# Fusing the recurrent r and z products of a GRU step into one product per column group

## The chip, the cores and the metric

The kernel runs on one core of a Trainium2 chip. The metric is the device time of one execution in microseconds; lower is better. Names of engines in what follows: PE is the matrix engine (its weight loads are listed apart, as PEld), DVE the vector engine, ACT the scalar engine, POOL the general engine, SP the engine that issues the DMAs.

## What is computed

The input `x` has 8 sequences of 512 positions and 256 channels. A mixture-of-experts layer with one shared and eight routed experts is added to it, and then a GRU-like recurrence runs over the 512 positions, whose outputs are added too:

```
x = x + moe(x, cond, ...)                 # per token, no recurrence
for t in range(512):                       # H is 8 x 256, H = cond at the start
    Z = sigmoid(x_t @ Wxz.T + bxz + H @ Whz.T + bhz)
    R = sigmoid(x_t @ Wxr.T + bxr + H @ Whr.T + bhr)
    H_tilda = tanh(x_t @ Wxh.T + bxh + (R * H) @ Whh.T + bhh)
    H = Z * H + (1 - Z) * H_tilda
    Y_t = H @ Whq.T + bhq
out = x + Y
```

The products with `x_t` need no earlier state and can be made a tile ahead. The products with `H` and `R * H` cannot: a step needs the state of the step before, and within a step the third product needs the first.

## The kernel before

The 512 positions are cut into NT = 32 tiles of TS = 16 steps. Two things run interleaved on the same engines. One is the recurrence, 512 steps in a row. The other is all the rest of the next tiles (experts up and down, routing, input projections) and the output product of the tile before; it is cut into small pieces, and tables written out by hand (`DOWNS1`, `UP_GAP2`, `ADD2`, `SILU1`, `HIDDEN1`, `BIASED1`, `ROUTE_AHEAD1` and others, indexed by a place r from 0 to 31 in a period of two tiles) say after which part of which step each piece is issued. Every engine has its own instruction stream in program order, and semaphores tie them together.

A state is 8 sequences by 256 channels. The channels are cut into NG = 4 groups of GW = 64, and each group sits in its own 32 partitions, of which 8 (B) are used. So r, z and c of one step are each a 128-partition by 64-column block of a PSUM bank, of which `NI` = 2 halves of Q = 32 columns are taken in turn by ACT and DVE. The step in program order:

- PE: `gate_product(r_ps, 0, hT, k)` for k = 0, 1 (the 256 channels of H are two contractions of 128), with 4 matmuls of 64 columns each, one for a column group of the array; it writes bank `r_bank`. Then the same for z into the first 64 columns of `zc_bank`. Then `fill_up`, a piece of the other work. Then, after a wait for `rhT_ready`, the same for c into columns 64 to 127 of `zc_bank`. Then `fill_rest`, more other work. All are made by line 1247. A float32 matmul is two records in the trace, so 8 matmuls show as 16 records. Where there is no other work left, `keep_busy` (line 1255) puts two matmuls there whose result nobody reads.
- ACT: tanh of r in two halves (`t_r`, line 693), tanh of z (`t_z`, line 695), the seed of the next step's r (`seed_r`, line 616: a copy of the precomputed input part from `xs` into `r_bank`, onto which the products accumulate), then `a_row` (line 704), an affine copy of `t_z` which waits for `tz_ready`. After c is done: tanh of c in two halves (`t_h`, line 713), then `seed_zc` (line 624), the seed of the next step's z and c, 128 columns. Then one piece of other work.
- DVE: transposes `t_r` (line 982, twice), makes `rhT` from it (line 985, twice), transposes `a_row` into `factors` (line 990), then a piece of other work in some steps, then `terms` from `factors` (line 1001), then transposes `t_h` into `terms` (line 1006, twice) and makes the new state with a scan into `hist` (line 1009, twice). Then another piece of other work in most steps.

Every tile ACT also copies the finished states (`keep_states`, line 631) right behind `a_row` of the tile's first step. SP stores and reloads the input parts by way of DRAM; two of its waits count the seeds of z and c, to know when the rows of `xs` may be overwritten. PSUM has 8 banks of 512 float32 columns, all used.

Of the kernel before, what the change touches and what calls it, by code (L numbers as in the profile page):

```python
# [17 lines left out]
def moe_then_gru(nc, x, cond, router_w, router_b, w1, w3, w2, we1, we2,  # L18
# [32 lines left out]
    with ctx:  # L51
# [84 lines left out]

        r_bank = ctx.enter_context(nc.psum_tensor("r_bank", [P, 512], F32))
        zc_bank = ctx.enter_context(nc.psum_tensor("zc_bank", [P, 512], F32))
        up_ps = [ctx.enter_context(nc.psum_tensor(f"up_ps{i}", [P, 512], F32)) for i in range(2)]
        dn_ps = [ctx.enter_context(nc.psum_tensor(f"dn_ps{i}", [P, 512], F32)) for i in range(2)]  # L140
        misc = ctx.enter_context(nc.psum_tensor("misc", [P, 512], F32))
        aux = ctx.enter_context(nc.psum_tensor("aux", [P, 512], F32))
        r_ps, z_ps, c_ps = r_bank[:, 0:GW], zc_bank[:, 0:GW], zc_bank[:, GW:2 * GW]
        tr_ps = [r_bank, zc_bank]

# [47 lines left out]
        xs_zeroed = sem("xs_zeroed")  # L193
        seeded_r = sem("seeded_r")
        seeded_zc = sem("seeded_zc")
        w13_high_ready = sem("w13_high_ready")
# [5 lines left out]
        hT_ready = sem("hT_ready")  # L202
        r_done = sem("r_done")
        z_done = sem("z_done")
        c_done = sem("c_done")
# [201 lines left out]
        def _(sp):  # L407
# [99 lines left out]
            def body(n, scan, proj, outs):  # L507
                if n % 2 == 0 and n > 0:
                    store_out(n - 2)
                if proj:  # L510
                    sp.wait_ge(xs_second, 16 * NG * (n + 1))
                    for q in range(PIECES):
                        store_inputs(n + 1, q)
                    sp.wait_ge(seeded_zc, TS * n + HALF)
                    for q in range(PIECES):
                        sp.wait_ge(xp_stored[q], 16 * (n + 2))
                        gate_rows(q, 0, xs_first)
                if n % 2 == 0 and 0 < n < NT:
                    store_out(n - 1)
                if proj:  # L520
                    sp.wait_ge(seeded_zc, TS * (n + 1))
# [35 lines left out]
        def _(act):  # L557
# [121 lines left out]
            act.wait_ge(xs_first, 16 * NG)  # L679
            seed_r(0, 0)  # L680
            seed_zc(0, 0)
            consume_up(1, 2)

            def body(n, scan, proj, outs):
                for s in range(TS):
# [3 lines left out]
                    if scan:  # L689
                        for i in range(NI):  # L690
                            if i == 0:
                                act.wait_ge(r_done, TS * n + s + 1)
                            act.activation(t_r[:, i, :], r_ps[:, i * Q:(i + 1) * Q], ACT.Tanh, scale=0.5).then_inc(tr_ready, 1)  # L693
                        act.wait_ge(z_done, TS * n + s + 1)
                        act.activation(t_z[:, :, :].rearrange("p i q -> p (i q)"), z_ps, ACT.Tanh, scale=0.5).then_inc(tz_ready, 1)
                    if after:
                        if s + 1 == HALF:
                            act.wait_ge(xs_second, 16 * NG * (n + 1))
                        if last:
                            act.wait_ge(xs_first, 16 * NG * (n + 2))  # L700
                        seed_r(*after)
                    if scan:
# [13 lines left out]
                    if after:  # L716
                        seed_zc(*after)
                    if 0 <= p < NPAIR and r in first_or(p, UP_ACT2_FIRST, UP_ACT2):
# [311 lines left out]
        def _(pe):  # L1030
# [41 lines left out]
            def set_bits():  # L1072

                pe.wait_ge(tr_act, (NTR + 1) // 2)
                pe.wait_ge(tr_dve, NTR // 2)
                for ps in (r_bank, zc_bank):

# [251 lines left out]
            def body(n, scan, proj, outs):  # L1329
                for s in range(TS):  # L1330
# [3 lines left out]
                    if scan:  # L1334
                        if (n, s) == (0, 0):
                            pe.wait_ge(seeded_r, 1)
# [44 lines left out]
```

## Time and profile before

| | us |
|---|---|
| median of 3 runs | 1278.86 |
| lowest and highest | 1277.06, 1281.6 |
| the profiled execution, its own time | 1277.44 |
| its span, first to last instruction | 1275.5 |
| granted clock of PE, share of full | 1.00 |
| PE matmul, PE weight load busy | 1249.8, 890.8 |
| DVE, ACT busy | 997.2, 803.3 |

The span holds a head of some 51 us, in which weights are loaded, split and transposed, and then the 512 steps until 1271 us. Busy time of PE counts a matmul from its first column to the write of its last, and matmuls overlap; so it says that something was in the array, not that the array was fed without a gap.

### The profile page before, as it was taken

Reading aid. Unit: us, or ns where it says so; the run is one execution under the profiler, and the core shown is the slowest. Engines: PE = TensorE matmul, PEld = TensorE weight load, DVE = VectorE, ACT = ScalarE, POOL = GpSimd, SP = SyncE. Lnnn points to the kernel's source line nnn. Section 1 sums busy time; section 2 is a strip of 40 time slices with the busy share of each in tenths; the row PEclk is TensorE's granted clock in tenths of the full one; section 3 lists DMA queues with packets and bytes.
Section 4 is the critical chain, followed back from the end, with each engine's and each line's share of the span. In section 5 each row is a group of like instructions: output and inputs, shape, how many; then the busy total and the mean of one; then the engine's idle time right before and its main releaser. Section 6 shows DMA issues by size and latency. Waiting matters only on the chain.

```text
span 1275.5 us, 84499 instructions
## 1 busy us (share of the span) xinstructions
PE 1249.8 (98%) x35704; PEld 890.8 (70%) x35704; DVE 997.2 (78%) x6111; ACT 803.3 (63%) x4402; POOL 7.4 (1%) x25
## 2 busy tenths in 40 slices
PE   9999999999999999999999999999999999999887
PEld 8877677766677776667776667776667776666554
DVE  6678888788787888878888787887877787877765
ACT  4366666666666666666666666666666666666554
POOL 1000000000000000000000000000000000000000
PEclk9999999999999999999999999999999999999999
DMA  8211011111101111011111101111011111001110
GB/s 273 57 36 43 24 38 30 42 41 34 36 24 39 38 37 45 24 37 27 44 39 35 38 21 41 35 39 45 27 33 27 44 39 33 23 21 27 33 32 11
DMA packets 76186, 51.34 MB, mean 40 GB/s; under 512 B 40609, under 2 KB 73761, under 8 KB 75809
## 3 DMA queue, kind: packets, MB, share of 16 engines
q1 hardware_dynamic: 75128, 45.29, 13.7%
q8 instruction: 281, 4.60, 1.5%
q14 instruction: 97, 0.79, 0.2%
q10 hardware_dynamic: 680, 0.66, 0.2%
HBM read 29.13 MB, written 16.78 MB: 36 GB/s over the span
## 4 chain that ended last, share of the span: by engine, by line
PE 93%; DVE 3%; ACT 2%; issue 1%; DMA 1%; SPq 0%
PE dn_ps L1083 27%; PE up_ps L1111 26%; PE zc_bank L1247 21%; PE r_bank L1247 14%; PE aux L1083 2%; DVE terms L1006 2%; PE dn_ps L1119 1%; ACT t_h L713 1%; PE misc L1083 1%; DVE hist L1009 1%; DMA x_all<-in_L_cond_W1e 1%; DVE t_rT L982 1%; ACT t_r L693 0%; DVE rhT L985 0%; SPq L411 0%
## 5 line engine op out<-in xcount | busy, mean ns | idle before, releaser
L982 DVE STREAM_TRANSPOSE t_rT<-t_r 128x32 f32<-128x32 f32 x1024 | 156.2, 191 | 171.1 <-ACT t_r L693 163.6
L693 ACT ACTIVATE t_r<-r_bank 128x32 f32<-128x32 f32 x1024 | 146.1, 195 | 210.2 <-PE r_bank L1247 200.2
L713 ACT ACTIVATE t_h<-zc_bank 128x32 f32<-128x32 f32 x1024 | 145.9, 195 | 207.7 <-PE zc_bank L1247 207.7
L1083 PE MATMUL dn_ps<-we_sb,x_all 128*32 128x256 f32 (+1 forms) x5144 | 274.5, 329 | 0.0
L1247 PEld LDWEIGHTS zc_bank<-whT,rhT 128*8 128x8 f32 x8192 | 118.1, 87 | 177.5 <-DVE rhT L985 176.9
L1247 PE MATMUL r_bank<-whT,hist 128*8 128x64 f32 x8192 | 210.1, 220 | 16.0 <-DVE hist L1009 13.4
L1247 PE MATMUL zc_bank<-whT,rhT 128*8 128x64 f32 x8192 | 211.0, 220 | 2.8 <-DVE rhT L985 0.3
L1247 PE MATMUL zc_bank<-whT,hist 128*8 128x64 f32 x8192 | 208.9, 219 | 0.8 <-issue 0.8
L1006 DVE STREAM_TRANSPOSE terms<-t_h 128x32 f32<-128x32 f32 x1024 | 156.5, 192 | 38.2 <-ACT t_h L713 19.7
L1247 PEld LDWEIGHTS r_bank<-whT,hist 128*8 128x8 f32 x8192 | 117.6, 88 | 94.6 <-DVE hist L1009 72.5
L1083 PEld LDWEIGHTS dn_ps<-we_sb,x_all 128*32 128x32 f32 x5144 | 137.9, 110 | 31.9 <-issue 1.0
L1111 PE MATMUL up_ps<-x_high,we_high 128*128 128x256 f32 (+1 forms) x540 | 159.1, 295 | 0.2 <-DVE hid L820 0.2
L1111 PE MATMUL up_ps<-x_high,we_low 128*128 128x256 f32 (+1 forms) x540 | 155.4, 288 | 0.0
L1111 PE MATMUL up_ps<-x_low,we_high 128*128 128x256 f32 x526 | 154.9, 294 | 0.0
L624 ACT ACTIVATE zc_bank<-gru_raw 128x128 f32<-128x128 f32 x512 | 144.3, 282 | 16.0
L1009 DVE TENSOR_TENSOR_SCAN hist<-factors,terms 128x16 f32<-128x16 f32 x1024 | 145.4, 184 | 0.0
L1247 PEld LDWEIGHTS zc_bank<-whT,hist 128*8 128x8 f32 x8192 | 142.4, 90 | 0.2
L990 DVE STREAM_TRANSPOSE factors<-a_row 128x64 f32<-128x64 f32 x512 | 126.0, 246 | 19.5 <-ACT a_row L704 1.4
L985 DVE SCALAR_TENSOR_TENSOR rhT<-t_rT,hist 128x8 f32<-128x8 f32 x1024 | 133.3, 168 | 0.0
L704 ACT ACTIVATE a_row<-t_z 128x64 f32<-128x64 f32 x512 | 125.7, 245 | 0.0
L852 DVE SCALAR_TENSOR_TENSOR x_all<-dn_ps,gates_all,x_all 128x256 f32<-128x256 f32 x256 | 121.3, 474 | 5.6 <-PE dn_ps L1119 1.9
L616 ACT ACTIVATE r_bank<-gru_raw 128x64 f32<-128x64 f32 x512 | 114.3, 223 | 3.4 <-DMA gru_raw<-gate_inputs_by_group 3.4
(132 smaller groups left out, 1691.4 us busy)
## 6 DMA issues: line engine op xcount, KB each, us to landing
gate_inputs_by_group<-gru_raw SPq DMA_DIRECT2D x64, 192.0 KB, 2.0
gru_raw<-gate_inputs_by_group SPq DMA_DIRECT2D x256, 48.0 KB
xT_all<-in_x SPq DMA_DIRECT2D x448, 8.0 KB
x_all<-in_x SPq DMA_DIRECT2D x31, 128.0 KB
out<-gru_raw SPq DMA_DIRECT2D x31, 128.0 KB
x_all<-in_L_cond_W1e SPq DMA_DIRECT2D x4, 512.0 KB, 7.6
we_sb<-in_L_cond_W2e SPq DMA_DIRECT2D x4, 512.0 KB, 8.6
xT_all<-in_L_cond_w SPq DMA_DIRECT2D x2, 256.0 KB, 5.3
```

Source lines behind the costliest of these rows:

```text
L624: act.activation(zc_bank[:, 0:2 * GW], xs[:, s, GW:RW], ACT.Copy).then_inc(seeded_zc, 1)
L693: act.activation(t_r[:, i, :], r_ps[:, i * Q:(i + 1) * Q], ACT.Tanh, scale=0.5).then_inc(tr_ready, 1)
L704: act.activation(a_row[:, :, :], t_z[:, :, :], ACT.Copy, bias=0.5, scale=-0.5).then_inc(a_ready, 1)
L713: act.activation(t_h[:, i, :], c_ps[:, i * Q:(i + 1) * Q], ACT.Tanh, scale=-1.0).then_inc(th_ready, 1)
L982: dve.transpose(t_rT[:, i, :], t_r[:, i, :]).then_inc(trT_done, 1)
L985: dve.scalar_tensor_tensor(rhT[:, i, :], t_rT[:, i, 0:B], 1.0, old[:, i, :], ALU.add, ALU.mult)\
L990: dve.transpose(factors[:, :, :, 1].rearrange("p i q -> p (i q)"), a_row[:, :, :].rearrange("p i q -> p (i q)"))\
L1006: dve.transpose(terms[:, i, :, 0], t_h[:, i, :]).then_inc(thT_done, 1)
L1009: dve.tensor_tensor_scan(hist[:, s, i, :, :].rearrange("p b e -> p (b e)"), factors[:, i, 0:B, :].rearrange("p b e -> p (b e)"), terms[:, ...
L1083: done = pe.matmul(ps[Q * j:Q * (j + 1), col:col + cols], lhsT[:, Q * j:Q * (j + 1)], rhs, start=first, stop=last, tile_position=(0, Q * j ...
L1111: done = pe.matmul(up_ps[place % 2][:, half * PAIR + begin * P:half * PAIR + end * P], w, (x_low if low_x else x_high)[:, p % 2, begin:end ...
L1247: done = pe.matmul(ps[Q * j:Q * j + B, :], lhsT[:, k, :], whT[:, gate, k, j * GW:(j + 1) * GW], start=False, stop=(k == NI - 1), tile_posi ...
```

## The change

The z block moves out of the bank that it shared with c and lies beside r: `rz_bank` holds r in columns 0 to 63 and z in 64 to 127, and `c_bank` holds c alone. The two products of 64 columns per column group and contraction half become one of 128 columns (its moving operand is two runs of 64 from `whT`). The seeds follow the banks: `seed_rz` copies 128 columns, `seed_c` 64, at the places where `seed_r` and `seed_zc` were. The product writes both gates, so there is one semaphore for them (`rz_done`), and the seed that overwrites both waits for both tanhs.

```
-        r_ps, z_ps, c_ps = r_bank[:, 0:GW], zc_bank[:, 0:GW], zc_bank[:, GW:2 * GW]
+        r_ps, z_ps, c_ps = rz_bank[:, 0:GW], rz_bank[:, GW:2 * GW], c_bank[:, 0:GW]
...
-            def seed_r(n, s):
+            def seed_rz(n, s):
                 if (n, s) == (0, 0):
                     act.wait_ge(bits_set, 2)
                 else:
                     act.wait_ge(tr_ready, NI * (TS * n + s))
-                act.activation(r_ps, xs[:, s, 0:GW], ACT.Copy).then_inc(seeded_r, 1)
+                    act.wait_ge(tz_ready, TS * n + s)
+                act.activation(rz_bank[:, 0:2 * GW], xs[:, s, 0:2 * GW], ACT.Copy).then_inc(seeded_rz, 1)
...
-            def seed_zc(n, s):
+            def seed_c(n, s):
...
-                act.activation(zc_bank[:, 0:2 * GW], xs[:, s, GW:RW], ACT.Copy).then_inc(seeded_zc, 1)
+                act.activation(c_ps, xs[:, s, 2 * GW:RW], ACT.Copy).then_inc(seeded_c, 1)
...
                             if i == 0:
-                                act.wait_ge(r_done, TS * n + s + 1)
+                                act.wait_ge(rz_done, TS * n + s + 1)
                             act.activation(t_r[:, i, :], r_ps[:, i * Q:(i + 1) * Q], ACT.Tanh, scale=0.5).then_inc(tr_ready, 1)
-                        act.wait_ge(z_done, TS * n + s + 1)
                         act.activation(t_z[:, :, :].rearrange("p i q -> p (i q)"), z_ps, ACT.Tanh, scale=0.5).then_inc(tz_ready, 1)
...
                         for k in range(NI):
                             pe.wait_ge(hT_ready, g + k + 1)
-                            done = gate_product(r_ps, 0, hT, k)
-                        done.then_inc(r_done, 1)
-                        pe.wait_ge(seeded_zc, TS * n + s + 1)
-                        for k in range(NI):
-                            done = gate_product(z_ps, 1, hT, k)
-                        done.then_inc(z_done, 1)
+                            for j in reversed(range(NG)):
+                                done = pe.matmul(rz_bank[Q * j:Q * j + B, 0:2 * GW], hT[:, k, :], whT[:, 0:2, k, j * GW:(j + 1) * GW],
+                                                 start=False, stop=(k == NI - 1), tile_position=(0, Q * j), skip_group_check=True)
+                        done.then_inc(rz_done, 1)
                     fill_up(p, r, scan)
                     if scan:
                         for k in range(NI):
                             pe.wait_ge(rhT_ready, g + k + 1)
                             if k == 0:
-                                pe.wait_ge(tz_ready, TS * n + s + 1)
+                                pe.wait_ge(seeded_c, TS * n + s + 1)
                             done = gate_product(c_ps, 2, rhT, k)
```

SP's two waits on `seeded_zc` become waits on `seeded_c` with the same counts; the names of the banks are exchanged where the head uses them for transposes.

## Rows read from the trace of the kernel before

**Rows 1.** Page, part 1: busy us (share of the span) and instructions
```profile
PE 1249.8 (98%) x35704; PEld 890.8 (70%) x35704; DVE 997.2 (78%) x6111; ACT 803.3 (63%) x4402; POOL 7.4 (1%) x25
```
**Rows 2.** Waits of the whole span: total us, times, longest us
```profile
ACT t_h L713 <- PE zc_bank L1247: 207.7, 481, 0.8
ACT t_r L693 <- PE r_bank L1247: 200.2, 379, 0.8
PEld zc_bank L1247 <- DVE rhT L985: 176.9, 509, 0.6
DVE t_rT L982 <- ACT t_r L693: 163.6, 434, 1.5
PEld r_bank L1247 <- DVE hist L1009: 72.5, 221, 1.0
```
**Rows 3.** Timeline, 627.7 to 630.0 us, one step: start us, length us, engine, line
```profile
627.70 0.41 PE L1247 MATMUL r_bank<-whT,hist 128*8 128x64 f32 x16
...
627.92 0.41 PE L1247 MATMUL zc_bank<-whT,hist 128*8 128x64 f32 x16
...
628.15 0.83 PE L1083 MATMUL dn_ps<-we_sb,x_all 128*32 128x256 f32 x16
628.17 0.28 ACT L693 ACTIVATE t_r<-r_bank 128x32 f32<-128x32 f32 x2 [0.60 <-PE r_bank L1247]
628.40 0.22 ACT L695 ACTIVATE t_z<-zc_bank 128x64 f32<-128x64 f32 x1
628.40 0.30 DVE L982 STREAM_TRANSPOSE t_rT<-t_r 128x32 f32<-128x32 f32 x2 [0.29 <-ACT t_r L693]
628.52 0.22 ACT L616 ACTIVATE r_bank<-gru_raw 128x64 f32<-128x64 f32 x1
628.65 0.26 DVE L985 SCALAR_TENSOR_TENSOR rhT<-t_rT,hist 128x8 f32<-128x8 f32 x2
628.66 0.25 ACT L704 ACTIVATE a_row<-t_z 128x64 f32<-128x64 f32 x1
...
628.87 0.41 PE L1247 MATMUL zc_bank<-whT,rhT 128*8 128x64 f32 x16
628.94 0.25 DVE L990 STREAM_TRANSPOSE factors<-a_row 128x64 f32<-128x64 f32 x1
629.11 0.13 DVE L776 TENSOR_TENSOR hit<-hit,rank 128x16 f32<-128x16 f32 x1
...
629.28 0.17 DVE L777 TENSOR_REDUCE best<-hit 128x2 f32<-128x16 f32 x1
...
629.35 0.28 ACT L713 ACTIVATE t_h<-zc_bank 128x32 f32<-128x32 f32 x2 [0.44 <-PE zc_bank L1247]
...
629.48 0.18 DVE L1001 SCALAR_TENSOR_TENSOR terms<-factors,hist 128x16 f32<-128x16 f32 x1
...
629.58 0.31 DVE L1006 STREAM_TRANSPOSE terms<-t_h 128x32 f32<-128x32 f32 x2
...
629.83 0.28 DVE L1009 TENSOR_TENSOR_SCAN hist<-factors,terms 128x16 f32<-128x16 f32 x2
```
**Rows 4.** Groups by form, whole span: busy us, mean ns of one record
```profile
L1247 PE MATMUL r_bank<-whT,hist 128*8 128x64 f32 x8192 | 210.1, 220 | 16.0 <-DVE hist L1009 13.4
...
L693 ACT ACTIVATE t_r<-r_bank 128x32 f32<-128x32 f32 x1024 | 146.1, 195 | 210.2 <-PE r_bank L1247 200.2
...
L1083 PE MATMUL dn_ps<-we_sb,x_all 128*32 128x128 f32 x2448 | 123.1, 273 | 0.0
...
L1083 PE MATMUL dn_ps<-wxT,x1T 128*32 128x384 f32 x992 | 103.0, 486 | 0.0
```
**Rows 5.** Timeline of ACT, 661.0 to 663.6 us, a step with `keep_states`
```profile
661.73 0.22 ACT L695 ACTIVATE t_z<-zc_bank 128x64 f32<-128x64 f32 x1
661.85 0.22 ACT L616 ACTIVATE r_bank<-gru_raw 128x64 f32<-128x64 f32 x1
661.99 0.25 ACT L704 ACTIVATE a_row<-t_z 128x64 f32<-128x64 f32 x1
662.14 0.64 ACT L631 ACTIVATE gru_raw<-hist 128x256 f32<-128x256 f32 x1
662.69 0.27 ACT L713 ACTIVATE t_h<-zc_bank 128x32 f32<-128x32 f32 x2
662.99 0.28 ACT L624 ACTIVATE zc_bank<-gru_raw 128x128 f32<-128x128 f32 x1
663.21 0.37 ACT L580 ACTIVATE gru_raw<-up_ps 128x256 f32<-128x256 f32 x1
```
**Rows 6.** Timeline of DVE: no wide operation, `shared_silu`, `shared_silu` at r = 9, two routing operations
```profile
653.07 0.17 DVE L1001 SCALAR_TENSOR_TENSOR terms<-factors,hist 128x16 f32<-128x16 f32 x1
653.35 0.31 DVE L1006 STREAM_TRANSPOSE terms<-t_h 128x32 f32<-128x32 f32 x2
...
724.57 0.16 DVE L1001 SCALAR_TENSOR_TENSOR terms<-factors,hist 128x16 f32<-128x16 f32 x1
724.73 0.30 DVE L1006 STREAM_TRANSPOSE terms<-t_h 128x32 f32<-128x32 f32 x2
...
660.41 0.16 DVE L1001 SCALAR_TENSOR_TENSOR terms<-factors,hist 128x16 f32<-128x16 f32 x1
660.53 0.31 DVE L1006 STREAM_TRANSPOSE terms<-t_h 128x32 f32<-128x32 f32 x2
...
631.87 0.18 DVE L1001 SCALAR_TENSOR_TENSOR terms<-factors,hist 128x16 f32<-128x16 f32 x1
631.96 0.31 DVE L1006 STREAM_TRANSPOSE terms<-t_h 128x32 f32<-128x32 f32 x2
```
**Rows 7.** Windows: the middle and a stretch without other work; busy us, then PEclk
```profile
200.00:1100.00 900.00, 896.82 (x26420) 636.80 (x26415) 723.40 (x4512) 584.81 (x3234) 0.00 (x0) 1.00 0.14 35
1235.00:1260.00 25.00, 20.12 (x566) 13.37 (x566) 15.82 (x108) 13.71 (x86) 0.00 (x0) 1.00 0.03 9
```

More of the change, by code:

```diff
@@ L135, in moe_then_gru @@
         hist = sb("hist", [P, TS, NI, B, 2])
-        r_bank = ctx.enter_context(nc.psum_tensor("r_bank", [P, 512], F32))
-        zc_bank = ctx.enter_context(nc.psum_tensor("zc_bank", [P, 512], F32))
+        rz_bank = ctx.enter_context(nc.psum_tensor("rz_bank", [P, 512], F32))
+        c_bank = ctx.enter_context(nc.psum_tensor("c_bank", [P, 512], F32))
         up_ps = [ctx.enter_context(nc.psum_tensor(f"up_ps{i}", [P, 512], F32)) for i in range(2)]
@@ L142, in moe_then_gru @@
         aux = ctx.enter_context(nc.psum_tensor("aux", [P, 512], F32))
-        r_ps, z_ps, c_ps = r_bank[:, 0:GW], zc_bank[:, 0:GW], zc_bank[:, GW:2 * GW]
-        tr_ps = [r_bank, zc_bank]
+        r_ps, z_ps, c_ps = rz_bank[:, 0:GW], rz_bank[:, GW:2 * GW], c_bank[:, 0:GW]
+        tr_ps = [rz_bank, c_bank]
         by_group = nc.dram_tensor("gate_inputs_by_group", [NG, P, RW], F32, kind="Internal").ap()
@@ L193, in moe_then_gru @@
         xs_zeroed = sem("xs_zeroed")
-        seeded_r = sem("seeded_r")
-        seeded_zc = sem("seeded_zc")
+        seeded_rz = sem("seeded_rz")
+        seeded_c = sem("seeded_c")
         w13_high_ready = sem("w13_high_ready")
@@ L202, in moe_then_gru @@
         hT_ready = sem("hT_ready")
-        r_done = sem("r_done")
-        z_done = sem("z_done")
+        rz_done = sem("rz_done")
         c_done = sem("c_done")
@@ L513, in body @@
                         store_inputs(n + 1, q)
-                    sp.wait_ge(seeded_zc, TS * n + HALF)
+                    sp.wait_ge(seeded_c, TS * n + HALF)
                     for q in range(PIECES):
@@ L520, in body @@
                 if proj:
-                    sp.wait_ge(seeded_zc, TS * (n + 1))
+                    sp.wait_ge(seeded_c, TS * (n + 1))
                     for q in range(PIECES):
@@ L679, in _ @@
             act.wait_ge(xs_first, 16 * NG)
-            seed_r(0, 0)
-            seed_zc(0, 0)
+            seed_rz(0, 0)
+            seed_c(0, 0)
             consume_up(1, 2)
@@ L700, in body @@
                             act.wait_ge(xs_first, 16 * NG * (n + 2))
-                        seed_r(*after)
+                        seed_rz(*after)
                     if scan:
@@ L716, in body @@
                     if after:
-                        seed_zc(*after)
+                        seed_c(*after)
                     if 0 <= p < NPAIR and r in first_or(p, UP_ACT2_FIRST, UP_ACT2):
@@ L1075, in set_bits @@
                 pe.wait_ge(tr_dve, NTR // 2)
-                for ps in (r_bank, zc_bank):
+                for ps in (rz_bank, c_bank):
                     pe.matmul(ps[:, 0:2 * GW], zeros[:, :], zeros[:, 0:2 * GW], start=True, stop=True).then_inc(bits_set, 1)
@@ L1335, in body @@
                         if (n, s) == (0, 0):
-                            pe.wait_ge(seeded_r, 1)
+                            pe.wait_ge(seeded_rz, 1)
                         for k in range(NI):
                             pe.wait_ge(hT_ready, g + k + 1)
-                            done = gate_product(r_ps, 0, hT, k)
-                        done.then_inc(r_done, 1)
-                        pe.wait_ge(seeded_zc, TS * n + s + 1)
-                        for k in range(NI):
-                            done = gate_product(z_ps, 1, hT, k)
-                        done.then_inc(z_done, 1)
+                            for j in reversed(range(NG)):
+                                done = pe.matmul(rz_bank[Q * j:Q * j + B, 0:2 * GW], hT[:, k, :], whT[:, 0:2, k, j * GW:(j + 1) * GW],
+                                                 start=False, stop=(k == NI - 1), tile_position=(0, Q * j), skip_group_check=True)
+                        done.then_inc(rz_done, 1)
                     fill_up(p, r, scan)
```

## The prediction

> **What bounds the kernel now.** The page's first part comes first, and it misleads: PE is busy 98% of the span, and DVE and ACT 78% and 63% [rows 1]. The waits say otherwise. PE's weight loader waited 509 times, once in nearly every one of the 512 steps, for `rhT` before the c product, 176.9 us in all; ACT waited 481 times for c and DVE 434 times for `t_r` [rows 2]. So the engines wait for each other in a ring. The timeline of one step gives the ring its numbers [rows 3]: r product starts at 627.70; `t_r` 628.17 (0.47 later); its transpose 628.40 (0.23); `rhT` 628.65 (0.25); c product 628.87 (0.22); `t_h` 629.35 (0.48); its transpose 629.58 (0.23); scan 629.83 (0.25). The next r product starts 0.24 to 0.25 behind the scan, since the ring from c to r costs 1.20 by the same kind of links. Sum: 1.17 from r to c and 1.20 from c to r, 2.37 to 2.38 us for a step. 512 steps of 2.38 are 1219 us, and with the head of 51 us and the last outputs this is the whole span. No link in the ring waits for anything but the one before it. The z product and the piece of other work stand on PE between r and c, and both fit: z runs from 627.92, the piece from 628.15, and c still starts 0.22 behind `rhT`, as it does in other steps. So z costs nothing today: it is streamed while ACT and DVE work on r.
>
> **Part 1: r is released later.** In the merged product the last record of r is also the last of z. How long is one pass? A record of 64 columns lasts 220 ns (by its name 128x64), one of 128 columns 273, one of 384 columns 486 [rows 4]. From 128 to 384 columns 213 ns are added in four steps of 64 columns: 53 ns for every 64 columns. The 16 records of r are four passes one after the other (four column groups of the array run beside each other): the r product starts at 627.70 and z at 627.92 [rows 3], so a pass of 64 columns takes 0.22 / 4 = 0.055 us. The merged product has four passes too (its 16 records are 2 halves of the contraction x 2 records x 4 groups), each 53 ns longer. Three lie before the last pass and the last is itself longer: 4 x 53.4 = 213.6 ns until `rz_done`. This is the z product, moved from behind the release of r to before it. Nothing in the ring gives it back, since `t_r` starts as soon as PE is done, and so do the transpose, `rhT` and c. 512 x 0.2136 = **109.4 us slower**. Bounds: if the two runs of 64 in the moving operand cost nothing more, that is the value; at 0.220 (the full length of four passes of 64, [rows 3]) it is 112.6, and at 4 x 0.0527 it is 107.9. No gain hides here unless PE itself were late for c in some steps, and 509 waits of 512 say that it is not [rows 2].
>
> What PE saves is small. The 16 weight-load and 16 matmul records of z go, but the columns stay: eight passes of 0.055 become four of 0.109, 0.44 us both. At most 0.01 us a step, and PE is not what the step waits for: nothing.
>
> The Trainium skill (TensorE: Matmul & The Clock Gate, Single matmul latency and Back-to-back issue gap) counts one cycle of 2.4 GHz for a column, 27 ns for 64 more, and a fixed 2.5 ns for every matmul, measured for bf16. By that page's figure the delay would be an estimated 4 x 27 = 107 ns a step and 55 us in all. This case's rows show 53 ns for 64 float32 columns in one record, so the trace disagrees and is used.
>
> **Part 2: the seed stands in the way of `a_row`.** ACT's order behind `t_r` is `t_z`, the next seed, `a_row`. Before, `t_z` starts 0.23 behind `t_r`, the seed of r 0.12 behind `t_z` without waiting for it, and `a_row`, which waits until `t_z` is written, 0.26 to 0.27 behind `t_z`: 0.49 behind `t_r` [rows 3, 5]. After, `t_z` has no wait and can follow at the pitch of two 32-column halves. That pitch is 0.28 - 0.195 = 0.09 (the pair takes 0.28 [rows 3], one 0.195 [rows 4]), so `t_z` is at 0.09 + 0.09 = 0.19. The seed covers both gates and must now wait until `t_z` is written, the same 0.265: it starts at 0.45. `a_row` follows a 128-column seed. The row nearest to that is ACT's other 128-column seed, from which the next instruction starts 0.22 later (662.99 to 663.21, [rows 5]). So `a_row` starts at 0.67 in place of 0.49, **0.18 later** against `t_r`. If the pitch grows only by the 64 columns that the seed has more (0.12 from `t_z` to the seed in rows 5, plus 0.05) it is 0.17 and the delay 0.14; if `t_z` doesn't come forward, the delay is 0.22. I take 0.18 and keep 0.14 and 0.22.
>
> Who waits? `factors` waits for `a_row` (628.66 to 628.94), the pieces of other work on DVE stand behind `factors`, `terms` (L1001) behind those, and the transpose of `t_h` (L1006) behind that. L1006 is in the ring. DVE can take it from 0.09 behind L1001's start (631.87 to 631.96 [rows 6], the least seen; 0.10 in rows 3). So the slack of a step is its distance from L1001 to L1006 less 0.09, and the loss is 0.18 less the slack. By kind of step:
> - Two routing operations between (r = 26 to 31, in 14 pairs of tiles: 84 steps): distance 0.10 or less, slack about 0.005 [rows 3]. 84 x 0.175 = 14.7 us.
> - `shared_silu` at r = 9 (15 steps): distance 0.12, slack 0.03 [rows 6]. 15 x 0.15 = 2.3 us.
> - One wide operation between (`shared_silu`, `shared_hidden` or `add_output_bias` at r = 3, 4, 5, 7, 11, 12, 19: seven places in 15 pairs, 105 steps): distance 0.16, slack 0.07 [rows 6]. 105 x 0.11 = 11.5 us.
> - Steps with none or one small operation: distance 0.28 and more, slack 0.19 [rows 6]. Nothing.
> - First steps of every second tile, where `keep_states` stands behind `a_row` and ends just in time: L631 at 662.14, `t_h` 0.55 behind it, with no wait for PE [rows 5]. It moves by 0.18 with `a_row`; 15 such steps, the others are among the routing steps above. 15 x 0.17 = 2.6 us.
>
> Sum **31 us**. At 0.14 it is some 21, at 0.22, where also the steps with a slack of 0.19 lose, some 44.
>
> **Part 3: what costs nothing.** The seed of c is 64 columns in place of 128, so ACT is free 0.05 us sooner behind `t_h`; it then has 0.2 us more than before until `t_r`, so nobody sees it. PE no longer waits for a seed between r and z, and its c product waits for `seeded_c`, which was issued a whole half step earlier (the seed follows `t_h` of the step before). SP's two waits get the same counts at nearly the same time, and the transfers behind them have half a tile to land. The pieces of other work on DVE and ACT behind the scan get 0.2 us more room; they delay nothing in the ring today, so nothing is gained.
>
> **Sum.** 1277.4 (the profiled execution; its span 1275.5) + 109.4 + 31 = 1418 us. That execution is 1.4 us below the median of the runs shown, so 1418 to 1419; I say 1418. A step goes from 2.38 to about 2.59 us, and to 2.77 in routing steps.
>
> **The rivals.**
> - *The ring alone.* The seed's detour stays within DVE's slack, because DVE can take `t_h`'s transpose later without loss or because ACT passes `a_row` sooner. Then only part 1 stands: 1277.4 + 109.4 = 1387, with a little of part 2 up to 1398. For it: most steps have 0.19 slack. Against: in 84 steps nothing is left between L1001 and L1006 [rows 3].
> - *Faster: PE is the bound.* If the 98% of rows 1 were a real limit, 16 fewer weight loads and 16 fewer matmul records a step would count. Eight passes of 0.055 to 0.056 become four of 0.109, at best 0.012 us a step, 6 us: 1271. It decides where PE's pieces end later than `rhT`; in this trace they ended before it in 509 of 512 steps [rows 2]. The Trainium skill (Perfetto Trace Analysis, Identifying the Most-Contended Engine) says that matmul busy time is a poor measure and that weight-load busy time is the better; here that is 70% [rows 1], and the waits agree with it.
> - *The clock falls.* PE idles about 0.22 us more in each step, before c. If the granted level went from 2.4 to 1.2 GHz, every pass of the ring would double: r and z 0.44, c 0.22 more a step and the pieces no longer fit, well over 1700. Against it: from 1235 to 1260 us there is no other work, PE's matmul records cover only 20.12 of 25 us and its weight loads 13.37, and the granted clock is 1.00, the level of 2.4 GHz [rows 7]. In the changed kernel the middle would be fuller than that.
> - *It doesn't do what it says.* If DVE or ACT were the bound already, moving r by 0.21 would be hidden in steps where `t_r` was late for another reason. 379 waits of ACT for r are counted [rows 2], fewer than 512; if the other 133 hid all of it, part 1 would be 81 us and the total 1389. The step starts don't support that: 0.47 from r to `t_r` [rows 3] is just three passes of 0.055, a record of 0.22 and some 0.08.
>
> **How the numbers follow.** My case as worked out, 1399 to 1432: 75%. The ring alone or hidden in part, 1380 to 1398: 14%. More than 1432 (part 2 at its upper bound with something queued behind it, or the clock): 8%. PE as the bound, 1271: 2%, and another 1% for anything within 0.3% of 1277, which is about what a measurement of this kernel can tell from no change. The range takes the first case and most of the second: 1392 to 1434.
>
> **What the changed kernel's profile would show.** The merged product's records last 273 ns, and `t_r` starts 0.68 behind its start in place of 0.47; r to c is 1.39 in place of 1.17. If it is 1.17, part 1 is wrong. c to r is 1.20 in steps without wide work on DVE; in routing steps it is 1.37 with L1001 and L1006 0.09 apart. If it is 1.20 everywhere, part 2 is wrong. `a_row` starts 0.67 behind `t_r`. PEld's wait for `rhT` grows by about 0.2 us a step, some 100 us. A granted clock below 1.00 would undo all of it.

## The result, and the profile after

The changed kernel takes 1424.5 us (median of 4 runs, 1423.6 to 1429.8) where the kernel before takes 1278.6 (4 runs): a ratio of 1.1146, 95% interval 1.1129 to 1.1163. It is 146 us slower. The profiled execution has a span of 1421.8 us.

Part 1 of its page answers rows 1. PE is busy for a smaller share (92%, its weight loads 62%) and has 8192 matmuls and 8192 weight loads fewer, which brought nothing:

```profile
PE 1309.2 (92%) x27512; PEld 883.8 (62%) x27512; DVE 967.7 (68%) x6111; ACT 835.8 (59%) x4402; POOL 7.4 (1%) x25
```

The waits (line that waited, line that released it, total us, times, longest) answer rows 2:

```profile
ACT t_r L693 <- PE rz_bank L1339: 378.2, 512, 1.2
PEld c_bank L1246 <- DVE rhT L984: 291.7, 512, 0.8
DVE t_rT L981 <- ACT t_r L693: 280.9, 510, 1.7
PEld rz_bank L1339 <- DVE hist L1008: 121.7, 367, 1.0
DVE factors L989 <- ACT a_row L703: 121.2, 483, 0.5
ACT t_h L712 <- PE c_bank L1246: 102.3, 459, 0.5
```

ACT now waits for the product in all 512 steps, 378 us against 200. The fifth line is new: `factors` waits for `a_row` in 483 steps, where before it waited in 3 of them, 1.4 us in all. That is part 2 of the prediction in one line. The same line of the kernel before:

```profile
DVE factors L990 <- ACT a_row L704: 1.4, 3, 1.0
```

One step with routing operations, as a timeline (start, length, engine, line), answers rows 3:

```profile
781.30 0.62 PE L1339 MATMUL rz_bank<-whT,hist 128*8 128x128 f32 x16 [0.16 <-DVE hist L1008]
...
781.74 0.83 PE L1082 MATMUL dn_ps<-we_sb,x_all 128*32 128x128 f32 x16
781.99 0.28 ACT L693 ACTIVATE t_r<-rz_bank 128x32 f32<-128x32 f32 x2 [0.35 <-PE rz_bank L1339]
782.16 0.23 ACT L694 ACTIVATE t_z<-rz_bank 128x64 f32<-128x64 f32 x1
782.22 0.31 DVE L981 STREAM_TRANSPOSE t_rT<-t_r 128x32 f32<-128x32 f32 x2 [0.88 <-ACT t_r L693]
782.47 0.26 DVE L984 SCALAR_TENSOR_TENSOR rhT<-t_rT,hist 128x8 f32<-128x8 f32 x2
782.48 0.28 ACT L616 ACTIVATE rz_bank<-gru_raw 128x128 f32<-128x128 f32 x1
...
782.69 0.41 PE L1246 MATMUL c_bank<-whT,rhT 128*8 128x64 f32 x16
782.70 0.24 ACT L703 ACTIVATE a_row<-t_z 128x64 f32<-128x64 f32 x1
782.97 0.24 DVE L989 STREAM_TRANSPOSE factors<-a_row 128x64 f32<-128x64 f32 x1 [0.24 <-ACT a_row L703]
...
783.16 0.29 ACT L712 ACTIVATE t_h<-c_bank 128x32 f32<-128x32 f32 x2 [0.22 <-PE c_bank L1246]
...
783.51 0.17 DVE L1000 SCALAR_TENSOR_TENSOR terms<-factors,hist 128x16 f32<-128x16 f32 x1
...
783.60 0.30 DVE L1005 STREAM_TRANSPOSE terms<-t_h 128x32 f32<-128x32 f32 x2
...
784.09 0.29 PE L1339 MATMUL rz_bank<-whT,hist 128*8 128x128 f32 x3
```

Product to `t_r` is 0.69 (0.47 before), product to c 1.39 (1.17), both as forecast. From `t_r` on to c nothing changed: 0.23, 0.25, 0.22. Behind c, `t_h` is 0.47 later (0.48 before), but its transpose stands 0.44 behind it, not 0.23, right behind `terms`, which is right behind the routing operations, `factors` and `a_row`. So c to the next product is 1.40 here against 1.20, and the step 2.79.

The form of the merged product answers rows 4 (count, busy us, mean ns):

```profile
L1339 PE MATMUL rz_bank<-whT,hist 128*8 128x128 f32 x8192 | 319.3, 274 | 42.3 <-DVE hist L1008 27.5
```

Taken over all steps of the two traces, the mean distance from the first product to c went from 1.177 to 1.387 (210 ns, 107.5 us in all), and that from c to the next step's first product from 1.205 to 1.281 (76 ns, 38.9 us; the expectations below have it as 38.7). Together 146 us. These two numbers are what the experiments have to account for.

### The profile page after: what moved, and what is told of

It is laid out like the page before. It is cut to its first block, busy times and chain, and to the rows that moved or that the text cites. A ratio compares the mean times of both kernels' runs of the same rounds, so it can differ in the third digit from the quotient of the medians.

```text
span 1421.8 us, 68563 instructions
## 1 busy us (share of the span) xinstructions
PE 1309.2 (92%) x27512; PEld 883.8 (62%) x27512; DVE 967.7 (68%) x6111; ACT 835.8 (59%) x4402; POOL 7.4 (1%) x25
## 4 chain that ended last, share of the span: by engine, by line
PE 49%; DVE 24%; ACT 20%; issue 5%; DMA 1%; ACTq 0%; SPq 0%; DVEq 0%
PE rz_bank L1339 23%; PE up_ps L1110 13%; ACT t_r L693 9%; PE c_bank L1246 7%; DVE t_rT L981 5%; ACT rz_bank L616 5%; DVE terms L1005 4%; DVE factors L989 4%; ACT a_row L703 3%; DVE hist L1008 3%; DVE terms L1000 2%; ACT t_z L694 2%; DVE rhT L984 2%; PE aux L1082 2%; PE dn_ps L1082 2%
## 5 line engine op out<-in xcount | busy, mean ns | idle before, releaser
L693 ACT ACTIVATE t_r<-rz_bank 128x32 f32<-128x32 f32 x1024 | 146.2, 195 | 378.2 <-PE rz_bank L1339 378.2
L1339 PE MATMUL rz_bank<-whT,hist 128*8 128x128 f32 x8192 | 319.3, 274 | 42.3 <-DVE hist L1008 27.5
L1246 PEld LDWEIGHTS c_bank<-whT,rhT 128*8 128x8 f32 x8192 | 117.1, 87 | 291.7 <-DVE rhT L984 291.7
L1246 PE MATMUL c_bank<-whT,rhT 128*8 128x64 f32 x8192 | 209.9, 220 | 64.1 <-DVE rhT L984 7.8
L1339 PEld LDWEIGHTS rz_bank<-whT,hist 128*8 128x8 f32 x8192 | 171.9, 89 | 131.0 <-DVE hist L1008 121.7
L712 ACT ACTIVATE t_h<-c_bank 128x32 f32<-128x32 f32 x1024 | 145.5, 194 | 104.4 <-PE c_bank L1246 102.3
L616 ACT ACTIVATE rz_bank<-gru_raw 128x128 f32<-128x128 f32 x512 | 143.9, 281 | 51.9 <-DMA gru_raw<-gate_inputs_by_group 3.6
L624 ACT ACTIVATE c_bank<-gru_raw 128x64 f32<-128x64 f32 x512 | 116.7, 228 | 16.0
L694 ACT ACTIVATE t_z<-rz_bank 128x64 f32<-128x64 f32 x512 | 118.8, 232 | 0.0
L1110 PEld LDWEIGHTS up_ps<-x_high,we_high 128*128 128x128 f32 x540 | 101.6, 188 | 12.4 <-DVE hid L819 0.3
```

Of the source, the lines that this page charges most:

```text
L616: act.activation(rz_bank[:, 0:2 * GW], xs[:, s, 0:2 * GW], ACT.Copy).then_inc(seeded_rz, 1)
L1110: done = pe.matmul(up_ps[place % 2][:, half * PAIR + begin * P:half * PAIR + end * P], w, (x_low if low_x else x_high)[:, p % 2, begin:end ...
L1246: done = pe.matmul(ps[Q * j:Q * j + B, :], lhsT[:, k, :], whT[:, gate, k, j * GW:(j + 1) * GW], start=False, stop=(k == NI - 1), tile_posi ...
L1339: done = pe.matmul(rz_bank[Q * j:Q * j + B, 0:2 * GW], hT[:, k, :], whT[:, 0:2, k, j * GW:(j + 1) * GW], start=False, stop=(k == NI - 1), ...
```

## Experiments

The theory on trial: a ring of latencies sets the time; it is longer by the z product, behind which r is now released (part 1), and by `a_row`, which the seed holds up (part 2). The rivals: the merged product or its bank is the cost; DVE would have hidden the order on ACT; PE's stream is the bound.

### The order on ACT

e1_arow_first:

```
                         act.activation(t_z...).then_inc(tz_ready, 1)
+                    if scan:
+                        act.wait_ge(tz_ready, TS * n + s + 1)
+                        act.activation(a_row...).then_inc(a_ready, 1)
                     if after:
...
                         seed_rz(*after)
-                    if scan:
-                        act.wait_ge(tz_ready, TS * n + s + 1)
-                        act.activation(a_row...).then_inc(a_ready, 1)
```

> The changed kernel with a_row issued ahead of the seed of r and z, everything else kept. Theory (ring plus detour): the 38.7 us by which c to r is longer than before come from a_row standing behind a seed that waits for t_z. With a_row first it starts 0.17 + 0.27 = 0.44 behind t_r (0.49 before the change, 0.71 after it), so these 38.7 us go. In 31 steps keep_states now stands behind the 128-column seed and starts 0.80 instead of 0.64 behind t_r, 31 x 0.15 = 4.7 us. 1424.5 - 38.7 + 4.7 = 1390 us. Rival (c to r is longer because the merged product or the banks disturb it, not the order on ACT): no change, 1424 us. Rival (DVE's slack would have hidden the order anyway and all is part 1): no change either.

Measured: 1390.3 us (ratio to before 1.0869, 1.0852 to 1.0885). Its timeline of ACT:

```profile
742.86 0.29 ACT L693 ACTIVATE t_r<-rz_bank 128x32 f32<-128x32 f32 x2 [0.87 <-PE rz_bank L1339]
743.03 0.23 ACT L694 ACTIVATE t_z<-rz_bank 128x64 f32<-128x64 f32 x1
743.30 0.26 ACT L697 ACTIVATE a_row<-t_z 128x64 f32<-128x64 f32 x1
743.46 0.26 ACT L616 ACTIVATE rz_bank<-gru_raw 128x128 f32<-128x128 f32 x1
```

`a_row` is 0.44 behind `t_r`, and 34 us are gone by swapping two instructions. Over all steps c to r comes back to 1.214 on average; what is left of part 2, 4.5 us, stands in the first steps of the tiles, where `keep_states` now follows the wider seed. Part 2 is shown: it was the order, and DVE did not hide it.

e2_one_wait, on the changed kernel:

```
                 else:
-                    act.wait_ge(tr_ready, NI * (TS * n + s))
                     act.wait_ge(tz_ready, TS * n + s)
```

> The changed kernel; the seed of r and z waits for t_z alone (which comes behind t_r on the same engine), so the separate wait instruction ahead of it is gone. Theory: the seed starts 0.265 behind t_z instead of 0.324, a_row 0.65 behind t_r instead of 0.71, which is 0.16 later than before the change instead of 0.22. By the slacks of the steps, which overstate the changed kernel's loss a little (44 worked out for 38.7 measured), the loss falls from 44 to 26: some 15 to 18 us less, 1407 to 1409 us. Rival (the second wait is free, the seed's delay has another cause): 1424 us.

Measured: 1407.9 us (1.101, 1.0992 to 1.1029), 16.6 less than the changed kernel. Where two waits are written ahead of one instruction, the trace has a semaphore instruction of its own for one of them. The changed kernel's trace lists it for line 615, the wait for `t_z`, in 511 steps (only 63 such in the kernel before):

```profile
L615 ACTq EVENT_SEMAPHORE  x511: 17/17/38, 51.9 to 1413.1; - x171
```

The first wait written (`tr_ready`) is carried by the seed itself, the second stands ahead of it. Here the second is the one that ends last, and the seed starts 0.32 behind `t_z` (782.16 to 782.48 above). With one wait it is 0.26:

```profile
900.31 0.23 ACT L693 ACTIVATE t_z<-rz_bank 128x64 f32<-128x64 f32 x1
900.57 0.28 ACT L615 ACTIVATE rz_bank<-gru_raw 128x128 f32<-128x128 f32 x1
900.79 0.24 ACT L702 ACTIVATE a_row<-t_z 128x64 f32<-128x64 f32 x1
```

This is the part of part 2 that the prediction did not have.

e6_seed_detour puts part 2 alone on the kernel before:

```
                     act.wait_ge(tr_ready, NI * (TS * n + s))
-                act.activation(r_ps, xs[:, s, 0:GW], ACT.Copy).then_inc(seeded_r, 1)
+                    act.wait_ge(tz_ready, TS * n + s)
+                act.activation(r_bank[:, 0:2 * GW], xs[:, s, 0:2 * GW], ACT.Copy).then_inc(seeded_r, 1)
```

> The kernel before, in which the seed of r is 128 columns wide and waits for t_z too, as in the change; 64 of its columns are never read. r is released as before. So this is part 2 alone, and larger than in the change, since t_z still comes 0.223 behind t_r: seed at 0.223 + 0.324, a_row 0.216 behind it, 0.76 instead of 0.49, 0.27 later. By the slacks of the steps this costs 61 to 66 us, and 5% less if it overstates as for the change: 1338 to 1344 us, with steps up to 0.27 longer where DVE has routing operations and 0.08 longer in the others. Rival (DVE hides it): 1279 us.

Measured: 1334.8 us (1.0432, 1.0416 to 1.0447), 54 us above before where 58 to 63 were expected with the 5% taken off. In all steps of its trace the distance from r to c has the mean 1.179, that of before (1.177), and from c to r 1.318 instead of 1.205, which is 57 us in all. The slacks alone had given 61 to 66, so they read 6 to 15% high. Two reasons are in the trace: where one wide operation stands ahead of `terms`, the transpose follows `terms` by 0.08, not 0.09 as assumed, and the scan follows the transpose by 0.240 (median) in place of 0.248.

### When r is released

e4_r_waits_for_z, on the kernel before:

```
                                 act.wait_ge(r_done, TS * n + s + 1)
+                                act.wait_ge(z_done, TS * n + s + 1)
                             act.activation(t_r[:, i, :], ...).then_inc(tr_ready, 1)
-                        act.wait_ge(z_done, TS * n + s + 1)
                         act.activation(t_z...)
```

> The kernel before, in which the tanh of r also waits for the z product; products, banks and seeds are as before. Theory (the time went because r is released with z, not because the product is merged): t_r starts 0.224 later in every step, 512 x 0.224 = 115 us, and a_row is not late, so nothing is added: 1278.6 + 115 = 1393 us, 7 us above e3 because two products of 64 columns take 0.01 us longer than one of 128. Rival (the wider product itself, its two runs or its bank, costs the time): 1279 us.

Measured: 1424.7 us (1.1138, 1.1122 to 1.1155): 32 us more than expected, and by chance the time of the changed kernel. The expectation failed by the same mechanism as above. The order of the two waits puts the late one, for z, in an instruction of its own, in every step:

```profile
L693 ACTq EVENT_SEMAPHORE  x512: 17/17/17, 51.5 to 1415.9; - x171
```

and from the first product to `t_r` it is 0.76, as the timelines of PE and of ACT show:

```profile
901.67 0.41 PE L1247 MATMUL r_bank<-whT,hist 128*8 128x64 f32 x16
901.90 0.41 PE L1247 MATMUL zc_bank<-whT,hist 128*8 128x64 f32 x16
```

ACT, same step:

```profile
902.43 0.28 ACT L694 ACTIVATE t_r<-r_bank 128x32 f32<-128x32 f32 x2 [0.59 <-PE zc_bank L1247]
```

e9_r_waits_for_z_alone has the one wait only (against the kernel before):

```
-                                act.wait_ge(r_done, TS * n + s + 1)
+                                act.wait_ge(z_done, TS * n + s + 1)
                             act.activation(t_r[:, i, :], ...).then_inc(tr_ready, 1)
-                        act.wait_ge(z_done, TS * n + s + 1)
                         act.activation(t_z...)
```

> As e4_r_waits_for_z, but the tanh of r waits for the z product only, with no second wait beside it. In e4 r to t_r was 0.760 us, 0.06 more than the 0.224 of z accounts for, and the wait for z stood in a semaphore instruction of its own ahead of t_r. Theory (that separate instruction, when its wait ends last, costs 0.06 in every step, 31 us): 1424.7 - 31 = 1393 us, r to c 1.40. Rival (a z product in the way costs 0.06 by itself): 1425 us.

Measured: 1391.3 us (1.0877, 1.0861 to 1.0893). Products of 64 columns, banks and seeds of the kernel before, and yet 112 us slower, only because r is handed on with z: r to c is 1.398 on average, c to r stays at 1.205. The merged product as such is not the cost.

e3_seeds_behind_th moves the seed of r and z from ahead of `a_row` to behind `t_h`, on the changed kernel:

```
-                    if after:
...
-                        seed_rz(*after)
                     if scan:
                         act.wait_ge(tz_ready, TS * n + s + 1)
...
                     if after:
...
+                        seed_rz(*after)
                         seed_c(*after)
...
-                        if (n, s) == (0, 0):
-                            pe.wait_ge(seeded_rz, 1)
+                        pe.wait_ge(seeded_rz, TS * n + s + 1)
                         for k in range(NI):
                             pe.wait_ge(hT_ready, g + k + 1)
```

> The changed kernel with the seed of r and z moved behind t_h, beside the seed of c, and PE waiting for it in every step. Theory: a_row is as in e1_arow_first and keep_states goes back to its old place, so part 2 is gone altogether: 1424.5 - 38.7 = 1386 us, which is before plus the delay of r alone (1278.6 + 107.5). The seed must be done within 0.72 us of t_h; it stands 0.19 behind it and takes 0.28, so PE does not wait for it. Rival (it does wait): each step grows by what it is late.

Measured: 1429.6 us (1.1177, 1.1158 to 1.1197), a miss of 44 us. The scan to the product was 0.34 in place of 0.25:

```profile
900.61 0.29 ACT L616 ACTIVATE rz_bank<-gru_raw 128x128 f32<-128x128 f32 x1
...
900.91 0.28 DVE L1007 TENSOR_TENSOR_SCAN hist<-factors,terms 128x16 f32<-128x16 f32 x2
...
901.25 0.62 PE L1337 MATMUL rz_bank<-whT,hist 128*8 128x128 f32 x16
```

The seed had ended at 900.90, as the scan began, so it was not late. The view of what the product waits for names it all the same ("ACT rz_bank L616: 85.1, 219"), which is a case of a release read off wrongly. e10_state_wait_first turns the two waits round (the edit against e3):

```
-                        pe.wait_ge(seeded_rz, TS * n + s + 1)
                         for k in range(NI):
                             pe.wait_ge(hT_ready, g + k + 1)
+                            if k == 0:
+                                pe.wait_ge(seeded_rz, TS * n + s + 1)
```

> As e3_seeds_behind_th, but PE's wait for the new state is written ahead of its wait for the seed. In e3 the scan to the product was 0.337 us instead of 0.246, with the wait for the state in a semaphore instruction of its own ahead of the first weight load. Theory (the late wait has to be the one that the weight load carries; the other, long over, costs nothing): 1429.6 - 512 x 0.091 = 1383 us, at most 1386. Rival (the seed is really late for PE): 1430 us as in e3.

Measured: 1383.6 us (1.082, 1.0804 to 1.0836). The 0.09 is gone (scan to product: mean 0.340 in e3, 0.248 here, 0.249 in the kernel before):

```profile
900.17 0.28 DVE L1007 TENSOR_TENSOR_SCAN hist<-factors,terms 128x16 f32<-128x16 f32 x2
...
900.42 0.34 PEld L1338 LDWEIGHTS rz_bank<-whT,hist 128*8 128x8 f32 x16 [0.27 <-DVE hist L1007]
900.42 0.62 PE L1338 MATMUL rz_bank<-whT,hist 128*8 128x128 f32 x16
```

This kernel is the change without part 2: its c to r is 1.203 on average, that of before. It is the best form of the merged product that was tried, and still 104 us slower than the kernel before: moving the seeds does not touch part 1.

### Columns or instructions

e5_no_z leaves the z product out of the kernel before:

```
-                        for k in range(NI):
-                            done = gate_product(z_ps, 1, hT, k)
-                        done.then_inc(z_done, 1)
```

The tanh of z waits for `seeded_zc` in place of `z_done`, and so does the c product.

> The kernel before without the z product (z is the tanh of its seed alone, so the state is another); all else is kept. It takes 16 weight loads and 16 matmul records, 0.22 us of PE's stream, out of every step, many more than the merge does. Theory (a ring of latencies, PE has room): nothing moves, 1277 to 1280 us. Rival (PE's stream is the bound, so that a merge saves time there): up to 512 x 0.22 = 115 us faster, 1164 us.

Measured: 1280.9 us against 1280.5, a ratio of 1.0008 (0.9997 to 1.0019). Two things cancel in that, and the trace keeps them apart. Up to 1230 us the granted clock is 1.00; in the last 40 us it falls:

```profile
1200.00:1230.00 30.00, 23.35 (x536) 12.84 (x524) 21.42 (x135) 16.84 (x105) 0.00 (x0) 1.00 0.11 32
1255.00:1272.00 17.00, 15.51 (x222) 9.72 (x218) 9.52 (x66) 8.30 (x52) 0.00 (x0) 0.60 0.04 10
```

The first 489 steps, all at the full clock, take 1162.8 us against 1165.3 before; the last 22 take 57.0 against 52.2. So with 16 matmul and 16 weight-load records a step less, PE gains at most 3 us where the rival asked for 115. That PE's stream is the bound is refuted.

e7_96_columns, on the changed kernel:

```
-  pe.matmul(rz_bank[Q * j:Q * j + B, 0:2 * GW], hT[:, k, :], whT[:, 0:2, k, j * GW:(j + 1) * GW], ...)
+  pe.matmul(rz_bank[Q * j:Q * j + B, 0:GW + Q], hT[:, k, :], whT[:, 0:2, k, j * GW:j * GW + 48], ...)
```

> The changed kernel with the merged product cut from 128 to 96 columns (48 of each gate's weights per group, so it computes something else); instructions and seeds are kept. Theory (columns cost, 53.4 ns for 64 in a pass): each of four passes is 26.7 ns shorter, 0.107 us a step, 54.7 us: 1370 us. Rival (the number of instructions costs): 1424 us.

Measured: 1376.0 us (1.0751, 1.0731 to 1.077), 48.5 less than the changed kernel and 6 above the expectation. The granted clock was not 1.00 to the end. Windows of this kernel (busy us of PE, PEld, DVE, ACT, POOL, then the clock):

```profile
1300.00:1313.00 13.00, 10.86 (x232) 5.50 (x224) 9.08 (x59) 7.46 (x43) 0.00 (x0) 1.00 0.05 18
1313.00:1346.00 33.00, 29.66 (x412) 18.24 (x412) 16.77 (x114) 15.91 (x92) 0.00 (x0) 0.60 0.09 24
1352.00:1370.00 18.00, 16.54 (x226) 10.21 (x218) 9.08 (x63) 8.53 (x51) 0.00 (x0) 0.59 0.03 9
```

e12_96_columns_busier doubles `keep_busy`:

```
-                for k in range(KC):
-                    done = pe.matmul(up_ps[0][:, 0:PAIR], w1_high[:, k, 0:P], x_high[:, 0, :, k, :], ...)
+                for k in range(2 * KC):
+                    done = pe.matmul(up_ps[0][:, 0:PAIR], w1_high[:, k % KC, 0:P], x_high[:, 0, :, k % KC, :], ...)
```

> As e7_96_columns, with four instead of two matmuls in each keep_busy, which stands only where no other work is left. In e7 the granted clock fell to half in two stretches of the last 60 us, and e7 took 1376 us where 1370 was worked out. Theory (those stretches are the 6 us): the clock stays at full and it is 1370 us, with the columns term at 0.107 us a step. Rival (the clock is not the cause, the columns term was too large): 1376 us; or the longer keep_busy delays c, which would be over 1376 us.

Measured: 1369.2 us (1.0712, 1.0694 to 1.073), and the same window of its profiled execution:

```profile
1313.00:1346.00 33.00, 29.44 (x545) 20.29 (x538) 19.31 (x132) 18.34 (x106) 0.00 (x0) 1.00 0.09 24
```

So 32 columns less, with as many instructions in the merged product, are worth 1424.5 - 1369.2 = 55 us, 0.108 us a step. The trace agrees: r to c has the median 1.283 in place of 1.388, 0.105 less, and c to r is the same. The columns are the cost, 26 to 27 ns for each 32 in a pass. That the clock was e7's 6 us shows in the steps too: the first 489 take as long in e7 as in e12 (1254.8 and 1254.3 us), the last 22 take 63.3 against 55.1.

### The other way round: releasing earlier

If a late release costs, an early one should gain. e8_c_in_halves cuts the c product of the kernel before in two:

```
+                        pe.wait_ge(seeded_c0, TS * n + s + 1)
                         for k in range(NI):
                             pe.wait_ge(hT_ready, g + k + 1)
...
-                            done = gate_product(c_ps, 2, rhT, k)
-                        done.then_inc(c_done, 1)
+                        pe.wait_ge(seeded_r, min(TS * n + s + 2, NT * TS))
+                        for i in range(NI):
+                            for k in range(NI):
...
+                                    done = pe.matmul((zc_bank if i else r_bank)[Q * j:Q * j + B, GW + i * Q:GW + (i + 1) * Q], rhT[:, k, :],
+                                                     whT[:, 2, k, j * GW + i * Q:j * GW + (i + 1) * Q], ...)
+                            done.then_inc(c_done if i else c0_done, 1)
...
+                act.activation(r_bank[:, GW:GW + Q], xs[:, s, 2 * GW:2 * GW + Q], ACT.Copy).then_inc(seeded_c0, 1)
```

> The opposite of the change, on the kernel before: the c product is cut in two of 32 columns per group in two banks (the first half in r's bank, the second beside z), with a seed of its own for the first half, so that ACT can take the first half of c while PE still makes the second. Theory (what counts is when the first half is released): the shortest passes in the trace are 31 ns (products of 8 columns), so the first half is released 0.07 us earlier than c is now, though the second comes 0.05 later; 512 x 0.07 = 38 us at most, less what DVE's slack (10 us or so) and PE's other work behind c (which then ends too late, 13 us or so) take back: 1255 to 1265 us. Rival (32 columns cost as much as 64, 56 ns a pass): the first half comes 0.03 earlier, the second 0.2 later, and PE's other work is pushed out: slower, 1300 us or more.

Measured: 1543.3 us (1.2057, 1.203 to 1.2085). The first expectation failed. The rival's "1300 us or more" holds, but not its reason: in the trace the 16 records of a half product take 0.30 us where those of 64 columns take 0.41, so 32 columns do cost less than 64. e11_halves_late_wait_first puts the late waits first (the edit against e8):

```
-                        pe.wait_ge(seeded_c0, TS * n + s + 1)
                             pe.wait_ge(hT_ready, g + k + 1)
+                            if k == 0:
+                                pe.wait_ge(seeded_c0, TS * n + s + 1)
...
-                        pe.wait_ge(seeded_r, min(TS * n + s + 2, NT * TS))
                                     pe.wait_ge(rhT_ready, g + k + 1)
+                                    if k == 0:
+                                        pe.wait_ge(seeded_r, min(TS * n + s + 2, NT * TS))
```

> As e8_c_in_halves, with the late waits (new state, r times state) written first in both products. Theory: the 0.09 us each of two late waits, 93 us, go: 1543 - 93 = 1450 us or less. What is left above the kernel before is then the cost of 32 more matmul and weight-load records a step in PE's stream, and no half product has been of use. If it comes down to about 1280, the halves were free and only the waits were the loss.

Measured: 1529.0 us (1.195, 1.1913 to 1.1986), a miss by 79 us. Its timeline of PE:

```profile
902.38 0.32 PE L1369 MATMUL r_bank<-whT,rhT 128*8 128x32 f32 x14
903.70 0.20 PE L1369 MATMUL r_bank<-whT,rhT 128*8 128x32 f32 x1 [1.00 <-issue]
903.71 0.21 PE L1369 MATMUL zc_bank<-whT,rhT 128*8 128x32 f32 x3
```

In the midst of a product PE stands still for 1.00 us with nothing to wait for, and 258 of the 511 distances from one step to the next are over 2.8 us; 12% of its chain is "issue", where the changed kernel has 5%. What PE stood still for is not in the view of the waits, but the table of DMA packets in the same trace has it. Queue 8 brings packets of 16 KB marked as instructions (packets, MB, share of 16 engines), here in the kernel before, the changed kernel and e11, in this order:

```profile
q8 instruction: 281, 4.60, 1.5%
q8 instruction: 218, 3.57, 1.1%
q8 instruction: 347, 5.69, 1.6%
```

From 200 to 1100 us PE and its weight loader start 256 records for each of these packets in every one of the three traces, so queue 8 carries PE's instructions. In e11 PE's weight loader stands still for more than 0.4 us without a releaser 257 times after the first 90 us, 215 us in all and 2.3 us at the longest, and 255 of these pauses end between 2 and 3.3 us after such a packet starts (median 2.5), a narrow window for packets that come 4.2 us apart. The pause above is one of them: the packet starts at 900.94 and ends at 902.14, and PE goes on at 903.70. The kernel before has 2 such pauses. So the trace points to PE running out of instructions: e11 has 43896 matmuls where before had 35704. No run tested this by itself, and why a kernel with 256 records every 4.3 us (before) doesn't pause is not settled.

The early release itself did happen. In an undisturbed step c starts at 899.99 and `t_h` 0.37 behind it, in place of 0.48:

```profile
900.36 0.20 ACT L723 ACTIVATE t_h<-r_bank 128x32 f32<-128x32 f32 x1 [0.35 <-PE r_bank L1369]
```

But the scan then stands 0.29 behind the transpose and the next product, at 901.20, 0.32 behind the scan, where both were 0.25 before (medians over all steps: 0.30 and 0.30). So c to r is 1.21, no shorter than before. What an early release is worth without these losses, no run shows. No kernel that was tried is faster than the one before.

## Why the prediction was right

The forecast was 1418 us, 1392 to 1434; it is 1424.5. By its steps:

- *What bounds the kernel.* Right. e5 took 0.22 us a step from PE, and the steps at the full clock became 5 ns shorter.
- *Part 1, 109.4 us.* Right. In a typical step the product to c grew from 1.175 to 1.388, the 213 ns that were worked out from the record lengths in rows 4. Over the whole trace it is 107.5 us, since a few steps of before were long for other reasons. The 104 us of e10 and 112 of e9 bracket it, with and without the merged product. e12 measured the price of columns by itself, 53 to 54 ns for 64. The Trainium skill's figure for 64 columns more (TensorE: Matmul & The Clock Gate, Back-to-back issue gap), an estimated 27 ns, would have given half; e12 shows that it can't be carried over to these float32 products.
- *Part 2, 31 us.* The mechanism was right, the size was off: the whole change has 38.9 us more between c and r, and 1424.5 - 1383.6 = 41 us by e10. The term that was mis-sized is the seed's wait. `t_z` at 0.19 behind `t_r` was 0.17, the seed's 0.22 ahead of `a_row` was 0.22 exactly, but the seed started 0.32 behind `t_z` in place of 0.265. So `a_row` came 0.22 later, not 0.18. That this is also the upper bound that the prediction kept (44 us) is chance: the bound was worked out for a `t_z` that does not come forward, and it did. e2 measured the difference alone: 16.6 us for the semaphore instruction, which leaves 22.7 us between c and r. So two errors partly cancel in the 31: the seed's wait was put too short, and the slacks read some 10% high, as e6 showed. By kind of step the 38.9 are 17.3 in the 84 with routing operations (14.7 forecast), 15.6 in the 120 with one wide operation (13.8), and 6.0 in all others (2.6), where at 0.22 the slack of 0.19 no longer covers steps that were put at nothing.
- *Part 3, nothing.* Right as far as the traces show: the sum of parts 1 and 2 leaves nothing over.
- *The rivals.* "The ring alone" (1387) is what e1 and e10 are, after the order was mended; in the change itself DVE did not hide the detour. "PE is the bound" fell with e5. "It doesn't do what it says" fell with the waits: ACT waits for the product in all 512 steps. The clock stayed: 1.00 over the changed kernel's stretch without other work, although its matmul records cover less of it (18.28 of 25 us) than before (20.12 of 25 in rows 7).

```profile
1394.00:1419.00 25.00, 18.28 (x370) 11.16 (x358) 14.19 (x96) 12.41 (x71) 0.00 (x0) 1.00 0.03 8
```

## What to carry to other kernels

In a ring of latencies, order the work so that the result which somebody waits for is released first, and let what nobody waits for be streamed behind it; merging two products saves instructions on PE and delays the first of them by the length of the second. When two results share a bank, whatever overwrites the bank waits for both, and everything queued behind it on that engine waits too: put the urgent instruction ahead of it. And of two waits ahead of one instruction, write the one that ends last first. Before a product is cut into more instructions, look in the trace at how many PE already takes in: e11 stood still for 215 us, where 38 us were hoped for from the earlier release.

## What the runs showed of the hardware

- Two waits ahead of one instruction are not one wait. In the four places looked at (line 615 of the changed kernel, 693 of e4, 1335 of e3, 1336 of e10) the one written later became a semaphore instruction of its own, and when it was the last to end it cost 0.06 us on ACT (e2: 16.6 us, felt in part of the steps; e4 to e9: 33 us in 512 steps) and 0.09 us on PE (e3 to e10: 46 us in 512 steps). When it had ended long before, it cost nothing that was seen (e10: scan to product 0.248, with one wait 0.249).
- In the last 60 us, where PE has only the recurrence and `keep_busy`, cutting the merged product by a quarter (e7) was enough for the granted clock to go to 0.60 over 33 us, a mix of its levels of 1.2 and 2.4 GHz; ahead of it PE's records had covered 10.86 of 13 us. Two more matmuls in each `keep_busy` held 2.4 GHz there and gave back 7 us. Without the z product (e5) it fell too, to 0.60 over 17 us; in the changed kernel it stayed at 1.00 with 18.28 of 25 us covered.
- With 43896 matmuls in place of 35704 (e8, e11) PE stood still without any wait, up to 2.3 us at a time in e11. One 16 KB packet of queue 8 goes with 256 of PE's records, and 255 of e11's 257 pauses of over 0.4 us end 2 to 3.3 us after such a packet starts.
